# Expert products and their weighing moved from the last phase into the steps of the attention phase

## What is computed

```python
gates = jax.nn.softmax(xf @ wg, axis=-1)
idx = jnp.argmax(gates, axis=-1)
loc = jnp.sum((jnp.cumsum(mask1, 0) - 1.0) * mask1, -1)     # place in its expert's queue
keep = loc < cap
h = jnp.einsum('ecd,edf->ecf', disp, w1) + b1[:, None, :]
y = (jnp.einsum('ecf,efd->ecd', h, w2) + b2[:, None, :])
out = jnp.where(keep[:, None], gate_val[:, None] * y[...], 0.0)
...
y1 = _ln(x + _mha(x, ...), ln1_g, ln1_b)
y2 = _ln(y1 + _moe(y1, ...), ln2_g, ln2_b)
x = x + y2
```

## Time and profile before

| | |
|---|---|
| median of 3 runs (lowest to highest) | 4943.64 us (4942.41 to 4948.22) |
| the profiled execution | 4948.74 us, span of its instructions 4947.0 us |
| busy over the span | PE 4053.3 us (82%), DVE 3187.6 (64%), ACT 1598.7 (32%), POOL 1589.3 (32%) |
| mean granted clock of PE | 0.856 of 2.4 GHz |
| the phases ahead | from 0 to 3969.8 us |
| attention phase | 3969.8 to 4499.6, 529.8 us |
| last phase | 4499.6 to 4947.0, 447.4 us |

### The profile page before, as it was taken

The page is one execution under the profiler, slowest core; times in us unless marked ns, Lnnn a source line. Parts: engine busy times, 40 slices in busy tenths (PEclk is TensorE's granted clock), DMA queues, the critical chain, the costliest instruction groups (busy, mean ns, idle before and its releaser), DMA issues. The chain is left out here.

```text
span 4947.0 us, 163276 instructions
## 1 busy us (share of the span) xinstructions
PE 4053.3 (82%) x66309; PEld 2968.2 (60%) x66309; DVE 3187.6 (64%) x6119; ACT 1598.7 (32%) x2983; POOL 1589.3 (32%) x2521
## 2 busy tenths in 40 slices
PE   6999999666389989899899898998999768885444
PEld 5666666433266767767677777776777656663221
DVE  3777777477466766667676666676765435553777
ACT  1222222144233434434344333343443223331000
POOL 1333333211044444444445444454454310000000
PEclk6999999889689999999999999999998755556677
DMA  0222222256312222222222222222222100002110
GB/s 23 50 57 43 43 55 51 48 142 156 107 36 48 52 44 46 48 53 48 50 43 51 46 48 46 46 56 46 47 51 45 26 18 18 18 18 60 32 32 23
DMA packets 677599, 243.70 MB, mean 49 GB/s; under 512 B 528088, under 2 KB 642464, under 8 KB 676512
## 3 DMA queue, kind: packets, MB, share of 16 engines
q1 hardware_dynamic: 668448, 229.56, 21.3%
q10 hardware_dynamic: 8448, 4.20, 0.3%
HBM read 150.70 MB, written 82.86 MB: 47 GB/s over the span
## 5 line engine op out<-in xcount | busy, mean ns | idle before, releaser
L1373 POOL TENSOR_TENSOR d_f<-d_ms,d_mhalf 128x16 f32<-128x16 f32 x64 | 239.5, 3743 | 959.3 <-DVE d_ms L1807 959.3
L1567 PE MATMUL d_pa<-d_wv,d_hs 128*128 128x512 f32 x1024 | 528.8, 665 | 0.7 <-DVE d_qk L1778 0.4
L1761 DVE SCALAR_TENSOR_TENSOR d_acc<-d_pa,d_cq,d_acc 128x512 f32<-128x512 f32 x576 | 431.7, 749 | 94.7 <-ACT d_acc L1406 79.7
L1383 POOL TENSOR_TENSOR d_prod<-d_ablk,d_tblk 128x15 f32<-128x15 f32 (+7 forms) x960 | 343.2, 357 | 220.1 <-DMA d_ablk<-a_blocks 149.1
L1387 POOL TENSOR_TENSOR d_tblk<-d_tblk,d_prod 128x28 f32<-128x28 f32 (+7 forms) x896 | 344.0, 384 | 70.7 <-POOL d_prod L1383 0.2
L1567 PEld LDWEIGHTS d_pa<-d_wv,d_hs 128*128 128x128 f32 x1024 | 222.9, 218 | 238.9 <-issue 227.2
L1542 PE MATMUL d_pa<-d_hq,d_wqk 128*128 128x259 f32 x768 | 250.8, 455 | 81.9 <-DVE d_acc L1761 59.0
L1580 PEld LDWEIGHTS d_pb<-d_of_head,d_sqT 128*128 128x128 f32 x2048 | 246.2, 196 | 39.1 <-issue 38.9
L1406 ACT ACTIVATE d_acc<-d_pa,d_cq 128x512 f32<-128x512 f32 x192 | 132.0, 688 | 412.7 <-PE d_pa L1542 409.8
L262 POOL TENSOR_TENSOR a_act<-a_act,a_cws 128x512 f32<-128x512 f32 x128 | 166.8, 1317 | 304.9 <-DMA a_cws<-cw_rows 155.9
L1370 POOL TENSOR_TENSOR d_nr<-d_n,d_half_power 128x16 f32<-128x16 f32 x64 | 186.9, 2921 | 204.7 <-DVE d_n L1846 192.6
(11 more groups left out here) (371 smaller groups left out, 9708.6 us busy)
## 6 DMA issues: line engine op xcount, KB each, us to landing
a_cws<-cw_rows SPq DMA_DIRECT2D x32, 1024.0 KB, 10.6
decays<-g_dec SPq DMA_DIRECT2D x16, 2048.0 KB, 7.3
d_dd<-decays SPq DMA_DIRECT2D x64, 512.0 KB, 4.0
d_hs<-h_t SPq DMA_DIRECT2D x512, 32.0 KB, 2.2
t_blocks<-d_tblk SPq DMA_DIRECT2D x128, 128.0 KB, 1.7
a_blocks<-d_at SPq DMA_DIRECT2D x512, 16.0 KB, 1.8
d_ablk<-a_blocks SPq DMA_DIRECT2D x64, 128.0 KB, 2.1
d_tt<-t_blocks SPq DMA_DIRECT2D x512, 16.0 KB, 1.9
```

The source lines that it names most:

```text
L1373: pool.tensor_tensor(f[:, :], ms[:, :], mhalf[:, :], ALU.pow).then_inc(sem("f_ready"), 1)
L1383: link(pool.tensor_tensor(prod[:, 0:n, 0:s + 1], ablk[:, s, s + 1:SB].unsqueeze(2).to_broadcast([P, n, s + 1]), tblk[:, 0, s, 0:s + 1].uns ...
L1567: last = pe.matmul(pa[:, B + m, :], hs[:, u % 2, t, :], wv[:, t, cols(m)], start=(t == 0), stop=(t == TAPS - 1))
L1761: last = dve.scalar_tensor_tensor(out=own, in0=raw(e)[:, :, t:t + QT], scalar=cq[:, t, col:col + 1], in1=own, op0=ALU.mult, op1=ALU.add)
```

## The change

The expert work that needs no counting is done in the attention phase. Step `i` of the new loop makes the attention of `i`, the projections of `i + 1`, finishes `i - 1`, and makes the expert products of `i - 2`, whose turned rows `yT` and gates `rt` are kept one step longer. The merged matrices are made behind step 0. Products come in eight halves (four experts, 512 columns each), all through one PSUM bank, `xp`; DVE weighs each half in one operation by the gates and puts it in `part`, and ACT puts the bias product beside it as a ninth plane; DVE's sum over nine planes gives `moe`, which is stored. The loop runs over two steps at a time, with steps -1 to 3 and 14 to 17 written out. The scores of the four heads go through the row groups in turn, and DVE softens two heads at a time. The last phase, now `capacity_phase`, only loads routes, `moe`, `y1` and `x`, makes one factor 0 or 1 for each token (`keep`) and does the second normalization, with three buffers and the statistics of the next sequence ahead of the scaling of this one. Cut to what matters, in the order PE, DVE, last phase:

```diff
-    ps = [ctx.enter_context(nc.psum_tensor(f"e_ps{n}", [P, 512], F32)) for n in range(8)]
+    part = sb("part", [P, NC, NE + 1, D])
+    xp = ctx.enter_context(nc.psum_tensor("e_xp", [P, 512], F32))
...
+            for i in range(-1, 2 * LOOP_FIRST):
+                iteration(0, i)
+            with engine.Fori(LOOP_FIRST, LOOP_LAST + 1) as p:
+                for q in range(2):
+                    iteration(p, q)
+            for i in range(2 * LOOP_LAST + 2, NU + 2):
+                iteration(0, i)
...
+                def experts(half):
+                    c, e0 = half // 2, NE // 2 * (half % 2)
+                    hold(sem("weighed"), HALVES * (i - 2) + half)
+                    pe.matmul(xp[:, :], yT[:, m % 2, c * P:(c + 1) * P], w12[:, e0:e0 + 4, :].rearrange("p e d -> p (e d)"),
+                              start=True, stop=True).then_inc(sem("products"), 1)
...
+                    for c in range(NC):
+                        here = slice(c * P, (c + 1) * P)
+                        for j in range(AH):
+                            rows = slice(AHD * j, AHD * j + AHD)
+                            last = pe.matmul(s4[j][:, here], qT[rows, here], kT[rows, here], start=True, stop=True)
+                    last.then_inc(sem("scores"), 1)
+                if past:
+                    hold(sem("on_ready"), i)
+                    hold(sem("route_ready"), i - 1)
+                    turn(on, sem("o_turned"))
...
+                turn_probs(0)
+                experts(2)
+                turn_probs(1)
+                experts(3)
+                turn_probs(2)
+                experts(4)
+                turn_probs(3)
+                experts(5)
...
+                attend(0)
+                attend(1)
+                experts(6)
+                attend(2)
+                attend(3)
...
+                def weigh(half):
+                    c, e0 = half // 2, NE // 2 * (half % 2)
+                    dve.wait_ge(sem("products"), HALVES * (i - 2) + half + 1)
+                    dve.tensor_tensor(part[:, c, e0:e0 + 4, :], xp[:, :].rearrange("p (e d) -> p e d", d=D),
+                                      rt[:, m % 2, 1, c, e0:e0 + 4].unsqueeze(2).to_broadcast([P, 4, D]), ALU.mult)\
+                       .then_inc(sem("weighed"), 1)
...
+                def reduce(c):
+                    if c == 0:
+                        wait(dve, sem("moe_stored"), 16 * NC * (i - 2))
+                        dve.wait_ge(sem("bias_taken"), i - 1)
+                    dve.wait_ge(sem("weighed"), HALVES * (i - 2) + 2 * c + 2)
+                    dve.tensor_reduce(moe[:, c, :], part[:, c, :, :].rearrange("p e d -> p d e"), AX_X, ALU.add)\
+                       .then_inc(sem("reduced"), 1)
...
-def linear_expert_phase(nc, x_in, y_in, route, x_out, w1_rows, b1_t, w2_rows, b2, ln_g, ln_b):
+def capacity_phase(nc, x_in, y_in, route, moe_in, x_out, ln_g, ln_b):
...
+            def gather(s):
+                n = s % BUFS
+                dve.wait_ge(sem(f"loaded{n}"), 48 * (s // BUFS + 1))
+                for c in range(NC):
+                    last = dve.scalar_tensor_tensor(out=mo[:, n, c, :], in0=mo[:, n, c, :], scalar=keep[:, s * NC + c:s * NC + c + 1],
+                                                    in1=yt[:, n, c, :], op0=ALU.mult, op1=ALU.add)
...
+            gather(0)
+            for s in range(NSEQ):
+                if s + 1 < NSEQ:
+                    gather(s + 1)
+                finish(s)
```

More of the change, by code:

```diff
@@ L2032, in _ @@
+            steps(pool, iteration)
         @block.scalar
         def _(act):
[L2034 to L2041, removed]
@@ L2043, in attend, with iteration, soften @@
-            def attend(u):
-                act.wait_ge(sem("max_ready"), u + 1)
-                for j in range(AH):
+            act.wait_ge(sem("weights"), SMALL)
+            def iteration(p, q):
+                i = 2 * p + q
+                n, k, m = q, q - 1, q - 2
+                now, then, past, main = have(p, n), have(p, n + 1), have(p, k), have(p, m)
+                def soften(j):
+                    if not now:
+                        return
+                    act.wait_ge(sem("max_ready"), 2 * i + j // 2 + 1)
@@ L2056, in mix @@
[L2056 to L2078, removed]
+                def turn(j):
+                    if not now:
+                        return
+                    act.wait_ge(sem("probs_turned"), AH * i + j + 1)
+                    act.activation(prT[:, j, :, :].rearrange("p c t -> p (c t)"), s4[j][:, :], ACT.Copy)\
+                       .then_inc(sem("prT_ready"), 1)
@@ new lines, in iteration @@
+                soften(0)
+                if main:
+                    act.wait_ge(sem("biases"), i - 1)
+                    act.activation(part[:, :, NE, :], tiles(turned), ACT.Copy).then_inc(sem("bias_taken"), 1)
+                soften(1)
+                soften(2)
+                turn(0)
+                soften(3)
+                turn(1)
+                turn(2)
+                turn(3)
+                if then:
+                    act.wait_ge(sem("h_turned"), i + 2)
+                    act.activation(hT[:, :], turned[:, :], ACT.Copy).then_inc(sem("hT_ready"), 1)
@@ L2087, in turn @@
                 last.then_inc(done, 1)
[L2089 to L2099, removed]
-                                     start=True, stop=True)
-                last.then_inc(sem("v_ready"), 1)
@@ L2163, in _ @@
+                if past:
+                    hold(sem("yT_ready"), i)
+                    for c in range(NC):
+                        last = pe.matmul(turned[:, c * NE:(c + 1) * NE], yT[:, k % 2, c * P:(c + 1) * P], wgs[:, :],
+                                         start=True, stop=True)
+                    last.then_inc(sem("logits"), 1)
+                if isinstance(p, int) and i == 0:
+                    merge_weights()
+            steps(pe, iteration)
         @block.vector
         def _(dve):
-            dve.wait_ge(sem("weights"), 16 * 8)
+            dve.wait_ge(sem("weights"), SMALL)
```

729 lines of the change are left out of this document (388 added, 341 removed).

## The result

The changed kernel took 4759.39 us (median of 4 runs, 4749.53 to 4765.61), the kernel before 4943.02 (4921.13 to 4948.22): a ratio of 0.9635, 95% interval 0.9602 to 0.9668. It is faster, as forecast, but by 184 us and not by 84, and 16 us under the lower end of the range.

The account below looks back on a forecast made before the run. Each phase was taken as a chain of hand-overs, PE busiest in attention at its lower clock, DVE bounding the last phase. 3969.8 + 768 + 125 = 4862.8, less 3.4 between span and median: 4859 us, range 4775 to 4915.

Parts of the forecast that it names:

- the two chains: Attention step: DVE's work up to the fifth weighing, 24.8 us, then PE's work from there to the logits, 19.2 us.
- full steps: Attention phase: thirteen steps with all parts, 44.0 us each where a step was 30.7, together 572 us.
- the phases ahead: Everything before the attention phase: taken as 3969.8 us from the profile of the kernel before.
- the last phase: After attention: 10 for routes, 9 set-up, 16 sequences of 6.35, 4 for the last store; 125 us where it was 447.4.
- PE at the lower clock: Attention step: PE stays at 1.2 GHz until the clock rises for k, v and logits; granted clock 0.5 to 0.65.
- Clock up in parts: Rival for the attention step: clock higher in some stretches, step 38 to 42.5 us, time 4781 to 4840; 14%.
- First part: Attention step from the end of the logits to the fifth weighing done, mostly DVE's work: 24.8 us.
- Second part: Attention step from half 5 through attend products, q, k and v to the logits, PE without a gap: 19.2 us.
- Scores "2.3": Attention step: 32 score instructions alternating over four row groups fall from 4.66 to about 2.3 us, so DVE starts at 2.3.
- The rival of the clock that never rises: Rival: k, v and logits also at the lower clock, 2.4 us more, step 46.4, time 4890; 13%.
- Every half exposed: Rival: DVE waits for the product at all eight weighings, step 51.4 us, time 4955; 6%.
- the power: Last phase: GpSimd's power in the normalization, 1.12 us of waiting, now lies under the next sequence's statistics.

Follow-up runs that it names:

- narrow_products: Each expert product multiplies 128 columns and not 512, weighing and sums still on 512, against the changed kernel: 4741.1 us (1 run) against 4759.4.
- double_products: Each expert product is made twice into the same bank, nothing else touched, against the changed kernel: 4758.9 us (1 run) against 4759.4.

## Why the prediction was wrong

The direction and the two chains were right; the clock at which PE's part of them ran was not, and the size was off by 100 us. Against the forecast span of 4862.8: full steps 13 x 5.93 = 77 us less, the other attention steps and edges 768 - 572 = 196 forecast and 681.7 - 494.9 = 186.8 measured, 9 less; the last phase 12 less; the phases ahead 3952.7 against 3969.8, 17 less. That makes the 115 between spans; 15 come back, as the median lies 11.7 above the profiled span and not 3.4 below.

- **The step that failed: "PE at the lower clock" from the end of the logits on through q**, with the range of 42.5 to 46 us for a step; what ran was a clock that goes up and down, 0.78 over the loop, and 38.1 us. Clock up in parts stood there as a rival with 14% and 38 to 42.5 us. With its 38.1 my sum gives 4859 - 77 = 4782, inside the range; that the time fell below 4775 is due to the other 23 us of the count above, mostly the phases ahead and the last phase. The argument against it, that transposes and 32-column products kept the clock at 0.51 before, was read from a step without the wide products among them; narrow_products shows 0.64 without their width, double_products 0.90 with twice their number.
- First part, 24.8 forecast, 22.0 measured. Routing 1.9 held. DVE's start at 2.3 came out by luck (4275.43 is 2.23 behind the logits' end at 4273.20): I had the scores end it, but they took 1.17 us and lay under routing, and 0.34 of idle DVE without a wait made up the time; in the next step DVE starts 1.84 behind the logits. The wait of 1.9 before the second weighing was not there: half 1 was ready, as PE was at the upper clock (no waits beside 4281.49, done at 9.0 where I had 11.1). From there to the fifth weighing 13.0 against 13.7.
- Second part, 19.2 forecast, 15.6 measured, gapless as forecast. Half 5 0.94 from start to start instead of 1.71, the first pair of attend products 2.53 instead of 3.44, turn y 0.43 instead of 1.1, q 1.26 instead of 1.71, v 0.89 instead of 1.38. The second pair of attend products, 3.27, and halves 6 and 7 were at the lower clock, as said, but half 6 took 1.85 and not 1.71: the earlier trace rows have 3.57 and not 3.42 for four such instructions.
- Scores "2.3" were 1.17, but routing covered it: worth 0.1 us here. Both of my figures, 2.3 and 1.5, divided the 4.66 of a stretch at 0.56, and part of that was the clock. At the upper clock the runs show 2.82 / 1.17 = 2.4 times for 32-row tiles of 128 columns, between my 1.9 and the 3.07 that the Trainium skill (TensorE: Matmul & The Clock Gate, Part 3: Packing small matmuls) gives for four tiles of 512 columns.
- DVE's costs held: weighing 0.69, sum 2.11 (forecast 2.17), 29.5 us of work a step. Of the places of the waits, those for halves 6 and 7 held; the second weighing never waited, and that of half 5, which my walk also had waiting, did in five steps of 13.
- The rival of the clock that never rises did not come: 0.78 in the loop with the single bank `xp`. I had put the Trainium skill (the same page, A second HAM failure mode: psum-queue depth-cycling) behind it, and that was a misreading: the section tells of a clock that oscillates between the two levels, not of one that stays low. An oscillating clock is what ran: after waits for that bank half 3 took 2.05 and half 4 1.10, and filling those waits gave 23 us in the full steps.
- Every half exposed did not come: 31 weighings of 104 waited (its sum has a slip, too: 8 x 2.07 is 16.6 and not 16.8).
- Last phase, 125 forecast, 113.3 measured: routes landed after 6.6 us and not 10; set-up 9.0 as said; 16 sequences of 5.88 (4652.67 to 4658.55) and not 6.35, in which DVE waited for something only once, for 0.2, so the power is covered, as said; 3.2 for the end. Transfers stayed hidden at a DMA share of 0.58.
- The phases ahead, with the same instructions, ended between 3940.4 and 3958.0 in the profiles of the changed kernel and of the twelve of the experiments, and at 3969.8 in that of before, the longest. A sum made against one execution carries that error of up to 30 us, and I had no term for it.

Open: why the clock falls in the attend products of one step and not of the next, with the same instructions behind the same waits. The runs show how often, not what decides it.

## What to carry to other kernels

When work is added to an engine that runs at its lower clock with gaps, price the step at both clocks, and don't take the level from a trace without the added work: here the clock rose from 0.56 to 0.78 and paid part of the cost back. Where two engines pass one buffer to and fro, put first what the other waits for, and everything that nobody waits for behind it: one exchanged pair of instructions gave 47 us in the full steps. A mean step can hide two kinds of step; list them one by one before explaining the mean. And where rounds of runs drift by 15 us, read what an edit is worth from the stretch that it touches as well as from the medians.

## What the runs showed of the hardware

- The same gapless stretch of 70 PE instructions took 10.9 us at a granted clock of 1.00 and 15.6 at 0.67; 16 attend instructions of 32 columns 1.87 against 3.46.
- Spare PE work in waits made kernels faster, by 42 us (4759.4 to 4717.0; 23 in the full steps) and by 26.5 (4687.1 to 4660.6; 19 in the full steps), although it computes nothing.
- Twice the 512-column products cost no time that can be told (4758.9 against 4759.4), and a quarter of their columns gained 18 us in one run, of which the full steps show 7.
- 32 instructions of 32 rows took 2.82 us row group by row group and 1.17 in turn, at the same clock.
